# Ternary weights of the feed-forward layer: W2's blocks compared, turned and stored in the second turn of the loop, W1's in the first, and the order of every turn rewritten

## The chip, the core and the metric

The kernel runs on one core of a Trainium2 chip. It is written in Bass with an explicit program for each engine: TensorE (PE), VectorE (DVE), ScalarE (ACT), GpSimd (POOL) and SyncE (SP), which issues all transfers. The engines meet through semaphores only, and each runs its own list in the order in which it is written. The metric is the device time of one execution in microseconds (us).

## The reference

A transformer block on `x` (8 sequences, 1024 positions, 512 channels, float32), with layer norms behind each half. The first half is segmented attention with a compressive memory over segments of 128 positions (8 heads of 64 channels):

```python
q, k, v = xs @ Wq, xs @ Wk, xs @ Wv          # by segment of 128 positions
sq = elu(q_s) + 1.0
att_mem = sq @ mem / (sq @ z)
sk = elu(k_s) + 1.0
mem = mem + einsum('bhlk,bhlv->bhkv', sk, v_s)
z = z + sk.sum(axis=-2)
att = softmax(q_s @ k_s.T * scale) @ v_s
att = gate * att_mem + (1 - gate) * att
x = layernorm(x + att @ Wo)
```

The second half is a feed-forward layer whose weights (W1 2048x512, W2 512x2048) are ternary:

```python
def _quantize(W):
    gamma = mean(abs(W))
    return clip(round(W / (gamma + 1e-5)), -1.0, 1.0)
h = relu(x @ _quantize(W1).T + b1)
x = layernorm(x + h @ _quantize(W2).T + b2)
```

## The kernel before

**Tiling.** There are 32 groups of work (`NG`); a group is one segment of 128 positions of two sequences (`TG = 2`; the two are called t = 0 and 1). The main loop of each engine runs g = 0 to 33 and is software-pipelined. A pass of it, here called a turn, handles three groups: q, k and v projections, scores, softmax and the product with v (`attend`) of group g; the output projection with Wo and the layer norm of group g-1 (`project_out`, `residual`, `normalise`); and the feed-forward layer of group g-2, except its first up projections, which stand ahead of that at the end of the turn before. Products are kept accurate by splitting float32 operands into a high and a low float16 part and adding three matmuls; splitting is what most of the work on DVE, ACT and POOL is (`qk_split`, `v_split`, `p_split`, `xt_lo`, `w_split`, `h_split` with `h_rest`).

**Banks.** PE's results go to eight PSUM banks. `ffn_up` alternates between banks 0 and 1, `ffn_down` accumulates in banks 6 and 7, all other jobs take banks 2 to 5 in rotation (`take`), and each waits until the bank's last user on another engine is done.

**Memory.** `read_memory(g, t)` multiplies sq of group g with the memory that group g-2 left; `update_memory(g, t)` multiplies sk and v of a group and `mem_add` on DVE adds the result. sk reaches its layout by transfers: DVE transposes 32x32 pieces, and then `move_sk` on SP moves them in 16 transfers of 32 KB. `move_att` and `move_y` do the same for the mixed attention (ahead of Wo) and the normalised rows (y, ahead of the feed-forward layer). So SP issues 48 such transfers a turn, besides x, results and the detour of the group's largest value over DRAM (`amax_dram`, `amax_row`). SP is one queue: what stands behind `move_y` waits for its 16 issues.

**The ternary weights.** W1 and W2 stay in float32 in parts of `w2t`, `w1t` and `arena` until their thresholds are known. They are turned in 32 blocks of 128x512, 16 of W1 and 16 of W2. For block n, `compare(n)` writes two float16 masks, `wbelow` (weight under minus the threshold) and `wabove`; `turn_w(n)` on PE multiplies each 128x128 piece with the identity and with minus the identity, which gives the transposed ternary block in bank n % 2; `put_w(n)` on ACT stores it in `w1t` or `w2t`. The masks lie in `yt`, which holds the transposed y from the end of the first turn on, four blocks deep. DVE makes both masks of even blocks and the `above` mask of odd ones; POOL makes the `below` mask of odd ones. Blocks 0 to 15 are turned at the end of turn 0, blocks 16 to 31 in turn 1 up to the second k projection, all in banks 0 and 1, and the first up projection waits for all of them:

```python
if n >= 2:
    pe.wait_ge(sem["relu"], n - 1)
else:
    pe.wait_ge(sem["wput"], NBLOCKS)
pe.wait_ge(sem["yt"], by_t(g, 1))
```

**Order.** It is written out by hand in the five `for g in range(NG + 2)` loops; there is no planner.

## Time and profile before

| quantity | value |
| --- | --- |
| median of 3 runs | 1914.51 us (1912.84 to 1919.87) |
| profiled execution | 1912.87 us |
| its span in the profile | 1910.9 us |
| busy share of the span: PE, DVE, ACT, POOL | 97%, 76%, 53%, 42% |
| mean granted TensorE clock | 0.991 of full speed |
| transfers | 117.49 MB, mean 61 GB/s, q1 busy 29.4% of 16 engines' span |

The profiled execution is 1.64 us under the median of the runs shown, and its span is 1.97 us shorter than its time. All stretches below are in us from the start of the span. Busy shares are averages over a loop in which an engine may wait in one place and be the limit in another, so the text reads stretches and single instructions beside them. An instruction's record in the timeline gives its start, its duration and in brackets how long the engine was idle ahead of it and what ended this wait.

### The profile page before, as it was taken

The page shows a single profiled execution, that of the slowest core. Times are in us where ns is not written, and L with a number is a line of the kernel's source. Part 1 is how long each engine was busy: PE and PEld are TensorE (multiplying, and loading weights), DVE is VectorE, ACT ScalarE, POOL GpSimd, SP SyncE. Part 2 cuts the span into 40 slices and gives each one's busy share as a digit, 9 for nine tenths or more (in the row PEclk, how much of TensorE's full clock was granted, in tenths as well). Part 3 has the DMA queues.
Part 4 walks back from the last instruction along what each step waited for, and adds up shares of the span by engine and source line. Part 5 has one row for each costly group of instructions (what it writes and reads, how often), then busy time and mean ns, then how long its engine had stood idle before and what let it go on. Part 6 is the DMA issues. An engine that isn't in the chain of part 4 may idle for free.

```text
span 1910.9 us, 44707 instructions
## 1 busy us (share of the span) xinstructions
PE 1855.7 (97%) x16575; PEld 1311.8 (69%) x16575; DVE 1449.1 (76%) x2969; ACT 1006.1 (53%) x2426; POOL 794.7 (42%) x790
## 2 busy tenths in 40 slices
PE   5689999999999999999999999999999999999998
PEld 3566677766777766677766677766677766677765
DVE  7867777777777787777777877777777777777774
ACT  5755555555554555554555554545555645555541
POOL 1813344443344444344444344444345444344443
PEclk9889999999999999999999999999999999999999
DMA  8412333223333233233223333323333322333110
GB/s 270 123 23 46 58 61 66 52 49 59 62 59 65 49 53 61 58 60 65 54 45 64 61 59 64 64 38 60 61 59 63 67 38 59 61 58 62 36 23 23
DMA packets 556422, 117.49 MB, mean 61 GB/s; under 512 B 529824, under 2 KB 533808, under 8 KB 555696
## 3 DMA queue, kind: packets, MB, share of 16 engines
q1 hardware_dynamic: 556208, 114.64, 29.4%
q8 instruction: 134, 2.20, 0.6%
q14 instruction: 80, 0.66, 0.2%
HBM read 50.54 MB, written 16.80 MB: 35 GB/s over the span
## 4 chain that ended last, share of the span: by engine, by line
PE 80%; SPq 7%; DVE 6%; DMA 3%; issue 2%; ACT 1%; POOL 1%; DVEq 0%; POOLq 0%; ACTq 0%
PE bank L431 12%; PE bank L430 12%; PE bank L444 8%; PE bank L445 8%; SPq L1551 7%; PE bank L280 6%; PE bank L282 6%; PE bank L281 6%; PE bank L413 3%; PE bank L411 3%; PE bank L412 3%; PE bank L368 3%; DMA amax_row<-amax_dram 2%; PE bank L294 2%; PE bank L347 2%
## 5 line engine op out<-in xcount | busy, mean ns | idle before, releaser
L430 PE MATMUL bank<-yt,w1t 128*128 128x256 f16 x2048 | 453.9, 273 | 0.0
L431 PE MATMUL bank<-yt,w1t 128*128 128x256 f16 x2048 | 453.9, 273 | 0.0
L1141 ACT ACTIVATE prob<-bank,exp_bias,gscalars 128x128 f32<-128x128 f32 x512 | 227.6, 455 | 356.6 <-DVE exp_bias L723 347.7
L444 PE MATMUL bank<-w2t,arena 128*128 128x512 f16 x1024 | 388.4, 379 | 0.0
L445 PE MATMUL bank<-w2t,arena 128*128 128x512 f16 x1024 | 388.1, 379 | 0.0
L1187 ACT ACTIVATE arena<-bank,b_scaled,wscalars 128x256 f32<-128x256 f32 x512 | 262.9, 569 | 213.4 <-PE bank L431 156.3
L858 DVE CAST arena<-arena 128x512 f16<-128x512 f32 x256 | 154.8, 605 | 89.9 <-ACT arena L1187 89.1
L1317 POOL TENSOR_TENSOR att_mem<-att_mem,gate_in 128x512 f32<-128x512 f32 x60 | 83.1, 1385 | 330.1 <-DVE att_mem L762 318.7
L430 PEld LDWEIGHTS bank<-yt,w1t 128*128 128x128 f16 x2048 | 200.5, 98 | 23.3 <-issue 0.3
L431 PEld LDWEIGHTS bank<-yt,w1t 128*128 128x128 f16 x2048 | 200.3, 98 | 22.7
L1395 POOL TENSOR_TENSOR arena<-arena 128x512 f16<-128x512 f32 x128 | 155.3, 1213 | 87.6 <-DVE arena L858 87.6
L444 PEld LDWEIGHTS bank<-w2t,arena 128*128 128x128 f16 x1024 | 100.1, 98 | 111.9
L445 PEld LDWEIGHTS bank<-w2t,arena 128*128 128x128 f16 x1024 | 100.2, 98 | 110.5
L1353 POOL TENSOR_TENSOR at<-att_dot,at 128x512 f16<-128x512 f32 x60 | 89.7, 1495 | 191.3 <-ACT at L1160 191.3
L673 DVE SCALAR_TENSOR_TENSOR xt<-x_blocks,gscalars,xt 128x512 f16<-128x512 f32 x62 | 83.3, 1343 | 84.7 <-ACT xt L1095 84.7
L280 PE MATMUL bank<-xt,wk_hi 128*128 128x256 f16 x512 | 141.0, 275 | 0.0
L281 PE MATMUL bank<-xt,wk_hi 128*128 128x256 f16 x512 | 140.6, 275 | 0.0
L282 PE MATMUL bank<-xt,wk_lo 128*128 128x256 f16 x512 | 140.6, 275 | 0.0
L280 PE MATMUL bank<-xt,wq_hi 128*128 128x256 f16 x512 | 139.5, 273 | 0.0
L282 PE MATMUL bank<-xt,wq_lo 128*128 128x256 f16 x512 | 139.5, 273 | 0.0
L281 PE MATMUL bank<-xt,wq_hi 128*128 128x256 f16 x512 | 139.5, 273 | 0.0
L718 DVE TENSOR_REDUCE row_max<-bank 128x4 f32<-128x512 f32 x128 | 87.4, 683 | 37.6 <-PE bank L317 37.6
(191 smaller groups left out, 4392.9 us busy)
## 6 DMA issues: line engine op xcount, KB each, us to landing
rows<-in_L_attn_x SPq DMA_DIRECT2D x32, 512.0 KB, 3.6
out_rows<-rows SPq DMA_DIRECT2D x64, 256.0 KB, 2.3
x_blocks<-in_L_attn_x SPq DMA_DIRECT2D x248, 64.0 KB, 2.8
sk<-sk_t SPq DMA_DIRECT2D x480, 32.0 KB, 2.0
att_dot<-att_mem SPq DMA_DIRECT2D x480, 32.0 KB, 2.0
y_blocks<-rows SPq DMA_DIRECT2D x480, 32.0 KB
arena<-in_L_ffn_W SPq DMA_DIRECT2D x6, 1024.0 KB, 5.5
w2t<-in_L_ffn_W SPq DMA_DIRECT2D x2, 1024.0 KB, 13.3
```

The source lines that it names most:

```text
L280: pe.matmul(ps[:, :, c], w_hi[n][:, k, cols], xt[:, :, k], start=k == 0, stop=False)
L281: pe.matmul(ps[:, :, c], w_hi[n][:, k, cols], xt[:, :, KT + k], start=False, stop=False)
L282: ins = pe.matmul(ps[:, :, c], w_lo[n][:, k, cols], xt[:, :, k], start=False, stop=k == KT - 1)
L430: pe.matmul(ps[:, c], w1t[:, k, cols], yt[:, g % 2, :, k], start=k == 0, stop=False)
L431: ins = pe.matmul(ps[:, c], w1t[:, k, cols], yt[:, g % 2, :, KT + k], start=False, stop=k == KT - 1)
L444: pe.matmul(banks[own][:], h_hi[:, f, toks], w2t[:, f, :], start=f == 0, stop=False)
L445: ins = pe.matmul(banks[own][:], h_lo[:, f, toks], w2t[:, f, :], start=False, stop=f == FT - 1)
L858: dve.tensor_copy(hi, h32[:, n % NH32]).then_inc(sem["h_hi"], 1)
L1141: ins = act.activation(prob[:, t, at], ps[:, c], ACT.Exp, scale=gcol(g, G_EXP), bias=exp_bias[:, t, at:at + 1], accum_out=row_sum[:, t, h: ...
L1187: ins = act.activation(h32[:, n % NH32, c * GT:(c + 1) * GT], ps[:, c], ACT.Relu, scale=w(H_SCALE_Y), bias=b1_scaled[:, f:f + 1])
L1395: pool.tensor_tensor(lo, h32[:, n % NH32], hi, ALU.subtract).then_inc(sem["h_pool"], 1)
L1551: sp.dma_start(to, at).then_inc(done, 16)
```

## The change

What it does:

- `compare(n)` runs on DVE alone, for both masks of every block. POOL's comparisons go. One semaphore, `masks`, counts finished blocks.
- The masks are two blocks deep instead of four and lie in `yt[:, 1]` only; `yt[:, 0]` is free for the y of group 0.
- Blocks 0 to 15 (W1) are still turned at the end of turn 0 through banks 0 and 1. Blocks 16 to 31 (W2) go through banks 6 and 7, which `ffn_down` does not need before turn 2: 16 to 19 behind the first k projection of turn 1, 20 to 23 behind its two `project_out`, ahead of `scores(1, 0)`, 24 to 27 behind `turn_p(1, 0, 0)`, and 28 to 31 in turn 2, ahead of `ffn_up(0, 3)`.
- The first up projection waits for the 16 stores of W1 alone; the first `ffn_down` waits for all 32.
- The order of the turns is rewritten on every engine and for all 34 turns. On PE three up projections of group g-1 and both `update_memory(g, ...)` close a turn; before, one up projection stood there and `update_memory(g - 1, ...)` stood behind `ffn_up(g - 2, 4)` of the next turn. On SP the gates' return, two of W2's loads and the x of groups 3 and 4 move from the end of turn 0 into turn 1.

The diff, cut to its core (of the rewritten loops it shows only the end of PE's and one place of SP's):

```diff
-        wbelow = yt[:, 0].rearrange("p t k n -> p (t k n)").rearrange("p (b n) -> p b n", b=4)
-        wabove = yt[:, 1].rearrange("p t k n -> p (t k n)").rearrange("p (b n) -> p b n", b=4)
+        masks = yt[:, 1].rearrange("p t k n -> p (t k n)").rearrange("p (m b n) -> p m b n", m=2, b=2)
+        wbelow, wabove = masks[:, 0], masks[:, 1]
...
+        def turned_bank(n):
+
+            return banks[n % 2 if n < NBLOCKS // 2 else 6 + n % 2][:].rearrange("p (j c) -> p j c", j=4)
+
...
             def turn_w(n):
 
-                ps = banks[n % 2][:].rearrange("p (j c) -> p j c", j=4)
+                ps = turned_bank(n)
                 if n == 0:
                     pe.wait_ge(sem["ident16"], 1)
                 if n >= 2:
                     pe.wait_ge(sem["wput"], n - 1)
-                pe.wait_ge(sem["above"], n + 1)
-                pe.wait_ge(sem["below_pool" if n % 2 else "below"], n // 2 + 1)
+                if n == NBLOCKS // 2:
+                    pe.wait_ge(sem["hscale"], 1)
+                    pe.wait_ge(sem["thr_chain"], 2)
+                pe.wait_ge(sem["masks"], n + 1)
                 for j in range(4):
                     cols = slice(j * P, (j + 1) * P)
-                    pe.matmul(ps[:, j], wabove[:, n % 4, cols], ident16[:], start=True, stop=False)
-                    ins = pe.matmul(ps[:, j], wbelow[:, n % 4, cols], minus16[:], start=False, stop=True)
+                    pe.matmul(ps[:, j], wabove[:, n % 2, cols], ident16[:], start=True, stop=False)
+                    ins = pe.matmul(ps[:, j], wbelow[:, n % 2, cols], minus16[:], start=False, stop=True)
                 ins.then_inc(sem["wturn"], 1)
 
             def project_qk(g, n, j):
...
                 else:
-                    pe.wait_ge(sem["wput"], NBLOCKS)
+                    pe.wait_ge(sem["wput"], NBLOCKS // 2)
...
+                if g == 0 and piece == 0:
+                    pe.wait_ge(sem["wput"], NBLOCKS)
...
                 ffn_up(g - 1, 0)
+                ffn_up(g - 1, 1)
+                ffn_up(g - 1, 2)
+                update_memory(g, 0)
+                update_memory(g, 1)
...
+                if n == 0:
+                    dve.wait_ge(sem["masks"], NBLOCKS)
...
-                if n >= 4:
-                    dve.wait_ge(sem["wturn"], n - 3)
-                if n % 2 == 0:
-                    dve.tensor_scalar(wbelow[:, n % 4], src, w(BELOW[m]), None, ALU.is_lt).then_inc(sem["below"], 1)
-                dve.tensor_scalar(wabove[:, n % 4], src, w(ABOVE[m]), None, ALU.is_gt).then_inc(sem["above"], 1)
+                if n >= 2:
+                    dve.wait_ge(sem["wturn"], n - 1)
+                dve.tensor_scalar(wbelow[:, n % 2], src, w(BELOW[m]), None, ALU.is_lt)
+                dve.tensor_scalar(wabove[:, n % 2], src, w(ABOVE[m]), None, ALU.is_gt).then_inc(sem["masks"], 1)
...
-                else:
+                elif g == 1:
                     act.wait_ge(sem["wturn"], NBLOCKS)
...
                     act.wait_ge(sem["hscale"], 1)
+                    act.wait_ge(sem["masks"], NBLOCKS // 2 + 4)
...
-            def compare(n):
-                m, i, b = block_place(n)
-                src = ffn_raw(m, i)[:, b * 512:(b + 1) * 512]
-                if n in (1, 17):
-                    pool.wait_ge(sem["threshold"], m)
-                pool.wait_ge(*ffn_raw_loaded(m, i))
-                if n >= 4:
-                    pool.wait_ge(sem["wturn"], n - 3)
-                pool.tensor_scalar(wbelow[:, n % 4], src, w(BELOW[m]), None, ALU.is_lt).then_inc(sem["below_pool"], 1)
...
                     last = 4 * i + 3
-                    sp.wait_ge(sem["above"], last + 1)
-                    sp.wait_ge(sem["below"], last // 2 + 1)
-                    sp.wait_ge(sem["below_pool"], last // 2 + 1)
+                    sp.wait_ge(sem["masks"], last + 1)
...
                 if g == 1:
+                    gates_back()
+                    load_ffn_w(2, 2)
                     load_ffn_w(2, 3)
```

What the rewriting moves on DVE, in three places. The first is the first turn, between the splits of the q projection and those of Wv's last part. `wv_lo` is the low part of Wv (two halves), `row_max` and `exp_bias` belong to the softmax of group 0; rows of before first, then of now.

```order
L890 SCALAR_TENSOR_TENSOR wv_lo<-arena,wscalars,wv_hi 128x4x256
L872 TENSOR_REDUCE wscalars<-bank 1x1
L874 TENSOR_SCALAR wscalars<-wscalars 1x1
L876 TENSOR_SCALAR wscalars<-wscalars 1x1
L878 TENSOR_SCALAR wscalars<-wscalars 1x1
L686 SCALAR_TENSOR_TENSOR q_lo<-bank,q_hi 128x2x256
L693 SCALAR_TENSOR_TENSOR sq_t<-exp_tmp,relu_tmp 128x2x256
L890 SCALAR_TENSOR_TENSOR wv_lo<-arena,wscalars,wv_hi 128x4x256
L884 COPY wscalars<-bank 128x1
L885 RECIPROCAL wscalars<-bank 128x1
L718 TENSOR_REDUCE row_max<-bank 128x4
```

```order
L692 SCALAR_TENSOR_TENSOR q_lo<-bank,q_hi 128x2x256
L699 SCALAR_TENSOR_TENSOR sq_t<-exp_tmp,relu_tmp 128x2x256
L898 SCALAR_TENSOR_TENSOR wv_lo<-arena,wscalars,wv_hi 128x4x256
L692 SCALAR_TENSOR_TENSOR q_lo<-bank,q_hi 128x2x256
L699 SCALAR_TENSOR_TENSOR sq_t<-exp_tmp,relu_tmp 128x2x256
L946 TENSOR_SCALAR gate_cols<-gate_cols 128x4
L948 RECIPROCAL gate_cols<-gate_cols 128x4
L950 TENSOR_SCALAR gate_cols<-gate_cols 128x4
L724 TENSOR_REDUCE row_max<-bank 128x4
L729 TENSOR_SCALAR exp_bias<-row_max,gscalars 128x4
L898 SCALAR_TENSOR_TENSOR wv_lo<-arena,wscalars,wv_hi 128x4x256
L608 TENSOR_REDUCE amax<-x_blocks 128x1
```

The one-element chain (L872 to L878) and its spread (L884, L885) now stand ahead of these rows, and both q splits, the gates' three operations and the first softmax maxima now stand ahead of Wv's second half, on which the v projection waits.

The second place is turn 1, where group 0's rows are normalised; L840 before and L846 now is `normalise`, L858 and L866 are `h_split` (the rounding of a piece of the feed-forward layer's h), L602 and L608 the group's largest value. In turn 1 that h belongs to no group yet, so the rows are those of turn 2 on. Before, then now:

```order
L822 SCALAR_TENSOR_TENSOR rows<-bank,gscalars,rows 128x512
L831 BN_STATS stats<-rows 128x6
L833 BN_AGGR mean_var<-stats 128x2
L858 CAST arena<-arena 128x512
L718 TENSOR_REDUCE row_max<-bank 128x4
L723 TENSOR_SCALAR exp_bias<-row_max,gscalars 128x4
L602 TENSOR_REDUCE amax<-x_blocks 128x1
L840 TENSOR_SCALAR rows<-rows,mean_var,rstd 128x512 x2
L718 TENSOR_REDUCE row_max<-bank 128x4
```

```order
L828 SCALAR_TENSOR_TENSOR rows<-bank,gscalars,rows 128x512
L837 BN_STATS stats<-rows 128x6
L839 BN_AGGR mean_var<-stats 128x2
L724 TENSOR_REDUCE row_max<-bank 128x4
L729 TENSOR_SCALAR exp_bias<-row_max,gscalars 128x4
L846 TENSOR_SCALAR rows<-rows,mean_var,rstd 128x512
L608 TENSOR_REDUCE amax<-x_blocks 128x1
L846 TENSOR_SCALAR rows<-rows,mean_var,rstd 128x512
L724 TENSOR_REDUCE row_max<-bank 128x4
L729 TENSOR_SCALAR exp_bias<-row_max,gscalars 128x4
L866 CAST arena<-arena 128x512
```

The `h_split` that stood ahead of the softmax maxima and `normalise` now stands behind the second pair of maxima, and one `normalise` goes ahead of the group's largest value, the other behind it.

The third place is the same turn ahead of the two `attend`. L847 before and L853 now are `turn_y`, which transposes y's pieces once `move_y` has landed; L732 and L738 are `p_split`, whose `pt_lo` `attend` needs; L739 and L745 invert the softmax sums; L615, L623, L621 and L629 are the scale of the next x. Before, then now:

```order
L739 RECIPROCAL inv_sum<-row_sum 128x8
L746 TENSOR_SCALAR dot_scale<-inv_sum,gscalars 128x8 x2
L847 STREAM_TRANSPOSE y_blocks<-y_blocks 128x512
L615 TENSOR_REDUCE gscalars<-amax_row 128x1
L732 SCALAR_TENSOR_TENSOR pt_lo<-bank,pt_hi 128x512
L623 TENSOR_SCALAR gscalars<-gscalars 128x1
L847 STREAM_TRANSPOSE y_blocks<-y_blocks 128x512
L732 SCALAR_TENSOR_TENSOR pt_lo<-bank,pt_hi 128x512
```

```order
L853 STREAM_TRANSPOSE y_blocks<-y_blocks 128x512 x2
L745 RECIPROCAL inv_sum<-row_sum 128x8
L621 TENSOR_REDUCE gscalars<-amax_row 128x1
L738 SCALAR_TENSOR_TENSOR pt_lo<-bank,pt_hi 128x512
L629 TENSOR_SCALAR gscalars<-gscalars 128x1
L745 RECIPROCAL inv_sum<-row_sum 128x8
L752 TENSOR_SCALAR dot_scale<-inv_sum,gscalars 128x8
L633 TENSOR_SCALAR gscalars<-gscalars 128x1
L738 SCALAR_TENSOR_TENSOR pt_lo<-bank,pt_hi 128x512
```

Both `turn_y` now stand together, ahead of the inverted sums, the scale's chain and the last three `p_split`; before, the second stood between `p_split` rows.

## Rows read from the trace of the kernel before

**Rows 1.** Busy time by stretch; columns in its first row (PEclk: granted clock).
```profile
core 0: us, PE busy (x) PEld busy (x) DVE busy (x) ACT busy (x) POOL busy (x), PEclk, DMA share, GB/s
120.00:131.00 11.00, 7.73 (x72) 6.67 (x73) 7.27 (x20) 6.90 (x22) 0.46 (x1) 0.53 0.26 46
300.00:400.00 100.00, 100.00 (x926) 72.63 (x924) 77.31 (x153) 52.40 (x126) 42.77 (x43) 1.00 0.31 59
```

**Rows 2.** Timeline of PE: the memory read between the two attends, in three turns.
```profile
357.68 0.33 PE L368 MATMUL bank<-mem,sq_t 64*128 64x65 f32 x2
414.44 0.33 PE L368 MATMUL bank<-mem,sq_t 64*128 64x65 f32 x2
1785.13 0.33 PE L368 MATMUL bank<-mem,sq_t 64*128 64x65 f32 x2
```

**Rows 3.** The waits of PE: line, releaser, us in total, times, longest.
```profile
PE bank L368 <- DVE pt_lo L732: 3.9, 11, 0.4
PE bank L265 <- POOL yt L1405: 2.8, 9, 0.6
```

**Rows 4.** SyncE issuing transfers: two turns, y by line (ns), the page for sk.
```profile
396.46 10.43 SPq L1551 DMA_DIRECT2D y_blocks<-rows  x16
407.63 12.00 SPq L1563 DMA_DIRECT2D sk<-sk_t  x16
453.22 14.46 SPq L1551 DMA_DIRECT2D y_blocks<-rows  x16
468.42 11.11 SPq L1563 DMA_DIRECT2D sk<-sk_t  x16
...
L1551 SPq DMA_DIRECT2D y_blocks<-rows x480: 585/611/4204, 167.7 to 1832.1; - x160
...
sk<-sk_t SPq DMA_DIRECT2D x480, 32.0 KB, 2.0
```

**Rows 5.** Timeline, VectorE and GpSimd, ahead of the transfer of y.
```profile
393.22 1.16 POOL L1395 TENSOR_TENSOR arena<-arena 128x512 f16<-128x512 f32 x1
393.30 1.10 DVE L723 TENSOR_SCALAR exp_bias<-row_max,gscalars 128x4 f32<-128x4 f32 x1
...
395.45 0.99 DVE L840 TENSOR_SCALAR rows<-rows,mean_var,rstd 128x512 f32<-128x512 f32 x2
...
397.17 0.23 DVE L723 TENSOR_SCALAR exp_bias<-row_max,gscalars 128x4 f32<-128x4 f32 x1
```

**Rows 6.** The memory updates by line, 340 to 480; min/median/max ns, first and last start.
```profile
L399 PE MATMUL bank<-v,sk x64: 220/222/271, 368.3 to 426.0; 128*64 128x65 f32 x64
```

**Rows 7.** Timelines of the start: VectorE, ScalarE, then PE to the first up projection.
```profile
39.47 1.27 DVE L890 SCALAR_TENSOR_TENSOR wv_lo<-arena,wscalars,wv_hi 128x1024 f16<-128x1024 f32 x1
...
41.68 1.13 ACT L1194 ACTIVATE wo_hi<-arena,wscalars 128x1024 f16<-128x1024 f32 x1
...
39.19 0.29 PE L313 MATMUL bank<-k_hi,q_hi 64*128 64x128 f16 x2 [3.54 <-DVE q_lo L686]
...
41.10 0.61 PE L294 MATMUL bank<-wv_hi,xt 128*128 128x512 f16 x1
...
87.44 0.27 PE L280 MATMUL bank<-xt,wk_hi 128*128 128x256 f16 x1
...
108.81 0.38 PE L411 MATMUL bank<-wo_hi,at 128*128 128x512 f16 x1
...
110.20 0.23 PE L313 MATMUL bank<-k_hi,q_hi 64*128 64x128 f16 x2
...
130.65 0.27 PE L430 MATMUL bank<-yt,w1t 128*128 128x256 f16 x1
```

**Rows 8.** The comparisons by line; durations are min/median/max in ns.
```profile
L913 DVE TENSOR_SCALAR yt<-w2t,wscalars x8: 469/478/903, 58.9 to 66.3; 128x512 f16<-128x512 f32 x8
...
L1405 POOL TENSOR_SCALAR yt<-arena,wscalars x12: 1717/1982/2355, 68.1 to 94.1; 128x512 f16<-128x512 f32 x12
```

**Rows 9.** The stores of the turned W1, ScalarE, same columns.
```profile
L1215 ACT ACTIVATE w1t<-bank x16: 587/597/617, 63.5 to 78.8; 128x512 f16<-128x512 f32 x16
```

More of the change, by code:

```diff
@@ L28 @@
     ident half ident16 ones bload bias_load b2_load
-    wmax wrow wchain wall wscale wsplit_hi wsplit wscaled wsplit_pool thr_row thr_all thr_chain threshold wsum above below below_pool
+    wmax wrow wchain wall wscale wsplit_hi wsplit wscaled wsplit_pool thr_row thr_all thr_chain threshold wsum masks
     wturn wput bias_turn bias_col bias_max bias_row bias_cell bias_all hs_chain hscale gate_exp gate_chain gate_cols gate_there gates
@@ L503, in _ @@
             for g in range(NG + 2):
-                ffn_up(g - 2, 1)
                 if g == 0:
                     turn_max(1)
-                ffn_up(g - 2, 2)
+                    turn_bias()
+                if g == 2:
+                    for n in range(28, 32):
+                        turn_w(n)
                 ffn_up(g - 2, 3)
+                if g == 1:
+                    sum_all(2)
                 if g == 0:
                     spread_max(1)
+                project_qk(g, "k", 0)
+                if g == 0:
+                    turn_max(2)
+                ffn_up(g - 2, 4)
+                if g == 0:
+                    spread_max(2)
                 if g == 1:
@@ L513, in _ @@
                         turn_w(n)
-                ffn_up(g - 2, 4)
-                update_memory(g - 1, 0)
-                update_memory(g - 1, 1)
+                ffn_up(g - 2, 5)
+                project_qk(g, "k", 1)
+                turn_att(g - 1, 0)
+                project_qk(g, "q", 0)
+                turn_att(g - 1, 1)
+                project_qk(g, "q", 1)
+                if g == 0:
+                    turn_max(3)
+                ffn_up(g - 2, 6)
+                if g == 0:
+                    spread_max(3)
+                ffn_up(g - 2, 7)
+                project_out(g - 1, 0)
+                project_out(g - 1, 1)
                 if g == 1:
@@ L519, in _ @@
                         turn_w(n)
-                project_qk(g, "k", 0)
-                if g == 0:
-                    turn_max(2)
-                ffn_up(g - 2, 5)
-                if g == 0:
-                    turn_bias()
+                scores(g, 0)
+                ffn_down(g - 2, 0, 0)
+                project_v(g, 0)
+                project_v(g, 1)
+                turn_p(g, 0, 0)
                 if g == 1:
@@ L575, in _ @@
                 if g == 0:
-                    for n in range(4, 8):
+                    for n in range(12, 16):
                         turn_w(n)
@@ L1023, in _ @@
                         compare(n)
-                invert_sums(g, 1)
-                scale_sums(g, 0)
-                scale_sums(g, 1)
+                read_scale(g, 0)
+                residual(g - 2, 0, 1)
                 turn_y(g - 1, 0)
+                if g == 0:
+                    scalars(0, 3)
+                turn_y(g - 1, 1)
+                if (g + 1) % (LIVE * NSEG) < LIVE and LIVE * NSEG <= g + 1 < NG:
+                    reset_memory((g + 1) // (LIVE * NSEG), place(g + 1)[2])
+                invert_sums(g, 0)
                 all_max(g + 1)
-                p_split(g, 0, 1)
-                x_scale(g + 1, 0)
                 if g == 0:
@@ L1033, in _ @@
                         compare(n)
-                turn_y(g - 1, 1)
+                p_split(g, 0, 1)
+                x_scale(g + 1, 0)
+                invert_sums(g, 1)
+                yt_lo(g - 1, 0)
+                scale_sums(g, 0)
+                x_scale(g + 1, 1)
                 if g == 0:
```

300 lines of the change are left out of this document (121 added, 179 removed).

## The prediction

> **What bounds the kernel now.** I read the page first: PE is busy 97% of the span, so the time is PE's list plus its gaps. The stretches say where gaps can be: between 300 and 400 us PE is busy all of 100.00 us at full clock while DVE has 77.31 and ACT 52.40, but from 120 to 131, just ahead of the first up projection, it is busy 7.73 of 11.00 at a granted clock of 0.53 [rows 1]. So a change of order can win or lose in two places: at the start, where PE waits, and in the few turns where the steady loop stalls.
>
> How much the loop stalls comes from one PE instruction seen turn by turn. The memory read starts at 357.68 and 414.44, a turn of 56.76 us, and 25 turns after the first it starts at 1785.13 [rows 2]. 25 undisturbed turns would be 1419.0, the trace has 1427.45: 8.5 us of stalls, about 10 over the whole loop (32 turns against 25 give 10.8; the early ones have no y to move, so I take 9.9). The list of waits has 3.9 us in 11 of them at that read, for DVE's `pt_lo` [rows 3]; the rest is at the attend just ahead. What makes DVE late is SP: moving y takes 10.43 us in a good turn and 14.46 in a bad one [rows 4], DVE waits in line for it (`turn_y`), and `p_split` stands behind that. A single issue of these 480 takes 0.611 us by the median and 4.2 at most [rows 4]: some issues are slow for a reason the order does not touch. I count 11 turns with a slow y.
>
> **The change, part by part.** All sums are made against the profiled execution, 1912.87 us (span 1910.9 and 2.0 around it); the median of the runs shown lies 1.64 higher, and I add that at the end.
>
> *Fewer blocks ahead of group 0's output projection.* A block is 8 matmuls of 128 columns. Six matmuls of 512 columns take 1.39 us from 108.81 to the scores at 110.20, 0.23 with the drain and 0.22 without [rows 7], so 128 columns take 0.055 and a block 0.44. Of blocks 16 to 31, twelve leave the stretch ahead of `project_out(0, ...)`: 12 x 0.44 = 5.3. PE's waits for POOL's masks, 2.8 us in 9 [rows 3], go too, since the masks come from DVE; I take 2.6 of them there. Group 0's output projection would end 7.9 earlier than the 110.20 of now, at 102.3, if everything ahead were unmoved; the next two paragraphs come out even on that point, since the stores that gate it lose 0.6 and the k projections gain this in the same wait.
>
> *The same work comes back.* Blocks 20 to 23 now stand ahead of `scores(1, 0)` and 24 to 27 ahead of `scores(1, 1)`. DVE needs two comparisons of 0.478 us for each block [rows 8], 0.96 against PE's 0.44, and the masks are two deep, so the last two of four blocks are waited for: 4 x 0.44 + 2 x (0.96 - 0.44), some more for ACT's store (0.60 [rows 9]) ahead of bank 6's reuse, in all 3.5 for the first four, and 1.4 for the second, whose masks are partly made while PE has other work. Lead left: 4.4 at `scores(1, 0)`, 3.0 at `scores(1, 1)`. I carry 3.1 to the first up projection, 130.65 [rows 7] to about 127.5: that stretch waits for normalise, its transfer and DVE, not for PE. Blocks 28 to 31 ahead of `ffn_up(0, 3)` give back 2.8: four blocks at 0.44 plus the masks' lag 1.04. Sum from there: -0.3.
>
> *DVE and the v projection of group 0.* The second half of Wv's split, now at 39.47, gets behind both q splits and the first softmax maxima, and the last q split behind ScalarE's two Wo halves of 1.13 [rows 7]. Scores move from 39.19 to about 41.5, they take 1.5, maxima and bias 1.0, the split 1.27: the v projection starts at 45.3 instead of 41.10, 4.2 late. It costs the stores 1.9 at their start (the first is at 63.5 [rows 9]) since a softmax group of four exponentials now goes behind the first four stores, and 0.6 at the end, which is the part already counted. If that cover is missing, the 4.2 go through to the end.
>
> *POOL's comparisons.* A comparison on POOL takes 1.98 us by the median, on DVE 0.478 [rows 8]. 16 more on DVE are 7.7 us; DVE has room for it in turn 1, where no feed-forward work of an older group exists, save in the masks' lag above. DVE's port is a cost the other way: `exp_bias` takes 1.10 us beside POOL's `h_rest` and 0.23 without it [rows 5]. So DVE's own comparisons get faster too: their longest is 903 ns, near double the median [rows 8].
>
> The Trainium skill ("Advanced Engine Details and Errata", VectorE Performance Modes, Mode Summary) says that VectorE's second SBUF port is shared with GPSIMD and that the two block each other; the 1.10 against 0.23 agrees. By that rule alone every comparison on DVE that took 903 ns beside POOL's would come to 478, and the start would gain where PE waits for masks; by the rows PE waits there for POOL's masks, which are counted already, so the sum stays.
>
> *The steady turn.* Two things pull against each other. First, `h_split` and the slow `exp_bias` stood ahead of `normalise` at 395.45 [rows 5]; with `h_split` behind, y's transfer is issued about 1.0 us earlier (0.87 of it the slow `exp_bias`; what `h_split` frees and what the group's maximum, now between the two `normalise`, takes are about equal). In slow turns the stall was about 0.9 (9.9 over 11), so nearly all of that goes: -9.9. Second, `update_memory` stands closer to the transfer it needs. Now five up projections of 16 matmuls of 256 columns (0.109 each, 1.745 together) lie between the attends and the update, which starts at 368.3, 10.7 behind the read at 357.68 [rows 2, 6]. After the change there are three: 10.7 - 3.5 = 7.2, so in the turn of 414.44 PE comes to the update at 421.6. sk lands then: y's issues start at 395.45, take 10.43, the gap to sk's is 0.74, sk's issues take 11.11 to 12.00 (11.4), and the last lands 1.4 behind their end (2.0 from an issue of 0.611) [rows 4]: 419.4. The margin is 2.1 us in a good turn. In a turn with a slow y the lateness over 2.1 is a wait on PE: 14.46 - 10.43 = 4.0 in the one shown, so 1.9 there, and 0.4 to 1.7 in the others, 10.6 in all. Net +0.7. Bounds: -9.9 if sk is never late, +25 if the margin is not there (below).
>
> *Tail.* The last two `normalise` and transfers of results are issued back to back; half an issue, +0.3.
>
> Nothing else has a price: SP's loads of W2 and of x move later into turn 1, where its queue has 11 us of room ahead of their use, and the wait of `ffn_down` for all 32 stores comes 10 us behind the last one. If either were late it would show as a wait of PE at `ffn_down(0, 0, 0)`, up to 3 us once.
>
> Sum: -0.3 + 0.7 + 0.3 = +0.7, 1913.6 for the profiled execution, and with the 1.64 of the medians 1915.2; I say 1915.0.
>
> **Rivals.** *Faster, 1903.* The lead of 7.9 is kept from Wo's end to the first up projection, as the comparisons run beside other work, less 2.8 for the last blocks, and a part of the stalls goes because slow issues have more room: -5.1 - 4.5 - 1.6 for a warm clock in the 11 us ahead of the first up projection [rows 1] is -11.2 from 1914.5, 1903. For it: the low clock there comes with PE's gaps, and shorter gaps end both. Against: that stretch waits for a chain of DVE and SP that the change moves by 1 us only.
>
> The Trainium skill ("TensorE: Matmul & The Clock Gate", Why this matters for your kernels) warns that idle gaps between bursts take TensorE back to half clock; the 0.53 from 120 to 131 agrees. Blocks strewn through turn 1 could by that rule fill gaps (the faster rival) or, where PE waits for masks ahead of them, make new ones.
>
> *Slower, 1937: `update_memory` waits for sk in every turn.* The place is PE's L405, the first matmul of the update at the turn's end. It decides as soon as the path of y and sk is over 2.1 us longer than I have it. A good turn's y at 10.43 and sk at 12.00 already take 0.6 of that; `yt`'s last reader, the x of the next group or 1.5 us of DVE's `sk_t` transpose behind `h_split` would take the rest. Then each turn is 0.8 to 0.9 longer, 28 turns: +24 on the profiled 1912.9, 1937. For it: sk's 16 issues begin where SP is free, so there is no slack in SP. Against: in the turn of 396.46 the margin is counted on real rows.
>
> *Slower at the start, about 1923.* DVE becomes the bound in turns 0 to 2: all 64 comparisons at 0.478 are 30.6 us on it, and PE at half clock ahead of the first up projection pays double for its own work: +8. This is inside "same" by the bound below.
>
> *The change does not do what it says:* the three banks' waits serialise the W2 blocks with `ffn_down`. No `ffn_down` exists before turn 2, so I give it nothing.
>
> **How the numbers follow.** About 0.5%, 9.6 us, is what a measurement of this kernel can tell from no change. The likeliest case (start about even, stalls traded) has 0.48, the start's rival with +8 has 0.08: 0.56 same. The faster rival has 0.21, the wait for sk in every turn 0.23. The range is 1902, just past the faster rival, to 1933, where the sk wait costs 0.6 a turn; the likeliest case alone spans 1908 to 1922.
>
> **What would show it.** The first up projection at 127.5 (130.65 before); v's projection at 45.3; no wait of PE for POOL in the turning of blocks; the memory read at a distance of 56.76 in good turns; no or few waits of the read for `pt_lo`; and waits of PE at the update for the transfer of sk, in about 11 turns and of 10 us in all. If that last number is over 25, the slower rival holds; if it is under 3 and the attends do not wait either, the faster one. A start later than 134 means that the comparisons on DVE, or v, set its end.

## The result

| | kernel before | changed kernel |
| --- | --- | --- |
| median of 22 runs each | 1915.62 us | 1919.78 us |
| lowest and highest | 1911.72, 1920.33 | 1916.16, 1923.48 |
| ratio, 95% interval | | 1.0021 (1.0013 to 1.0030) |
| profiled execution, span | 1912.87, 1910.9 | 1917.00, 1915.0 |
| mean granted clock | 0.991 | 0.990 |

The change makes the kernel slower by 0.21%, 4.2 us. It is under the 0.5% that the prediction took for no change, and with 22 runs on each side it is clear of zero. The two profiled spans differ by 4.1 us, so the trace pair can be read for where they go. The memory read between the attends marks three stretches:

| | before | after | difference |
| --- | --- | --- | --- |
| v projection of group 0 | 41.10 | 46.03 | +4.9 |
| first store of a W1 block | 63.5 | 68.4 | +4.9 |
| last store of a W1 block starts | 78.8 | 82.4 | +3.6 |
| output projection of group 0 ended, next work of PE | 110.20 | 107.51 | -2.7 |
| first scores of turn 1 | 110.20 | 110.52 | +0.3 |
| first up projection | 130.65 | 132.21 | +1.6 |
| memory read of turn 2 | 185.75 | 190.86 | +5.1 |
| the same 28 turns later | 1785.13 | 1787.56 | +2.4 |
| end of the span | 1910.9 | 1915.0 | +4.1 |

In this pair of profiles the start loses 5.1, the loop gives back 2.7, the last turns lose 1.7. A second pair (experiments 5 and 6) has +2.2, -5.1 and +1.6 for the three: single profiles, which show where time goes, while the 4.2 us is the medians'.

### The profile after

The busy time by stretch, which answers to [rows 1]; the second stretch holds the first three up projections:

```profile
core 0: us, PE busy (x) PEld busy (x) DVE busy (x) ACT busy (x) POOL busy (x), PEclk, DMA share, GB/s
120.00:131.00 11.00, 6.88 (x86) 5.68 (x85) 8.71 (x22) 7.64 (x24) 0.00 (x0) 0.81 0.34 83
132.20:137.50 5.30, 5.30 (x46) 4.47 (x44) 5.26 (x7) 2.33 (x5) 2.54 (x2) 0.86 0.22 36
300.00:400.00 100.00, 99.89 (x927) 72.90 (x926) 79.74 (x163) 52.50 (x122) 45.12 (x45) 1.00 0.32 60
```

The clock ahead of the first up projection is 0.81 where it was 0.53, but the next stretch still has 0.86: from 132.21 to the memory update at 138.27 the three up projections take 6.1 us, in the turn of 361.34 5.3 (363.09 to 368.43). The loop is as full as before; DVE has 2.4 us more in these 100 us.

The start, which answers to [rows 7] and [rows 9]; DVE, then SyncE, ScalarE and its stores by line, then PE, and last its waits from 64.9 to 107.2:

```profile
41.73 1.92 DVE L950 TENSOR_SCALAR gate_cols<-gate_cols 128x4 f32<-128x4 f32 x1
...
45.95 0.34 SPq L1495 DMA_DIRECT2D arena<-in_L_ffn_W  x1
46.34 0.44 SPq L1499 DMA_DIRECT2D gate_dram<-gate_cols  x1
47.09 0.33 SPq L1511 DMA_DIRECT2D amax_dram<-amax  x1
57.48 0.32 SPq L1518 DMA_DIRECT2D amax_row<-amax_dram  x1
57.85 0.47 SPq L1495 DMA_DIRECT2D arena<-in_L_ffn_W  x1
...
66.05 1.91 ACT L1212 ACTIVATE rows<-arena 128x2048 bf16<-128x2048 f32 x1 [2.09 <-DMA arena<-in_L_ffn_W]
...
L1222 ACT ACTIVATE w1t<-bank x16: 586/597/632, 68.4 to 82.4; 128x512 f16<-128x512 f32 x16
...
46.03 0.59 PE L300 MATMUL bank<-wv_hi,xt 128*128 128x512 f16 x1 [3.50 <-issue]
...
107.51 0.22 PE L271 MATMUL bank<-ident,yt 128*128 128x128 f16 x1 [0.53 <-DVE yt L920]
...
110.52 0.23 PE L319 MATMUL bank<-k_hi,q_hi 64*128 64x128 f16 x2
...
132.21 0.40 PE L436 MATMUL bank<-yt,w1t 128*128 128x256 f16 x1
...
PE bank L271 <- ACT w1t L1222: 3.7, 3, 2.2
PE bank L271 <- DVE yt L920: 2.9, 11, 0.4
```

The gates' last tiny operation takes 1.92 us at 41.73, and the v projection follows Wv's split at 46.03. On SyncE, the load of W2's second part (57.85) is issued right behind the return of the group's maximum (57.48), and ScalarE's last sum starts at 66.05 after 2.09 us of waiting for this load. All 16 stores of W1 are behind that sum. The first W2 blocks on PE's way to the scores begin at 107.51, where the output projection has ended; the scores start 3.0 us later. The last two lines are waits inside the blocks ahead of that, for ScalarE's stores and for VectorE's masks. In the kernel before, the same stretch has 0.9 us of waits for stores, 2.8 for GpSimd's masks and 1.5 more at the same line (L265) with no releaser named.

The reads of memory, which answer to [rows 2]:

```profile
361.34 0.33 PE L374 MATMUL bank<-mem,sq_t 64*128 64x65 f32 x2
418.11 0.33 PE L374 MATMUL bank<-mem,sq_t 64*128 64x65 f32 x2
1787.56 0.33 PE L374 MATMUL bank<-mem,sq_t 64*128 64x65 f32 x2
```

A good turn is 56.77 us long as before. From the read of turn 2, 28 turns take 1596.70 us; 28 of 56.765 would be 1589.42. The excess is 7.3, where the kernel before has 9.96 (1599.38). Without their excess the two spans are 1900.9 and 1907.7, in the second pair 1902.1 and 1906.0. Taken from the medians of 22 runs (less the 2.0 us outside the span), that leaves about 12 us of stalls for the kernel before and 11 for the changed one. This is an estimate, and by it the loop gives back about 1 us, less than either pair shows.

The waits of PE from 140 us on, which answer to [rows 3]:

```profile
PE bank L405 <- issue: 3.9, 7, 0.8
PE bank L417 <- DVE at L806: 1.3, 1, 1.3
...
PE bank L388 <- issue: 0.8, 2, 0.4
PE bank L405 <- DVE att_dot L780: 0.8, 1, 0.8
```

The waits for `pt_lo` at the read (L368 before, L374 now), 3.9 us in 11, are gone from the list. In their place PE waits 4.7 us in 8 at the memory update (L405) and 0.8 at the attend. The list names no releaser for 7 of the 8 (`issue`), but in 9 of the 28 turns the update starts 0.09 us after sk's last transfer has landed; in the turn of 361.34, which is not held up, it starts 1.97 us after it (368.43 and 366.46). L417 is the last group's `project_out`: VectorE's `at_lo` now comes behind one `h_split` more, 1.3 us once, which is most of the tail's loss.

VectorE ahead of y's transfer, which answers to [rows 5], then SyncE, which answers to [rows 4]:

```profile
396.77 0.54 DVE L846 TENSOR_SCALAR rows<-rows,mean_var,rstd 128x512 f32<-128x512 f32 x1
...
398.35 0.54 DVE L846 TENSOR_SCALAR rows<-rows,mean_var,rstd 128x512 f32<-128x512 f32 x1
...
399.63 0.23 DVE L729 TENSOR_SCALAR exp_bias<-row_max,gscalars 128x4 f32<-128x4 f32 x1
399.76 0.42 DVE L866 CAST arena<-arena 128x512 f16<-128x512 f32 x1
```

```profile
398.92 10.42 SPq L1526 DMA_DIRECT2D y_blocks<-rows  x16
410.08 12.99 SPq L1538 DMA_DIRECT2D sk<-sk_t  x16
L1526 SPq DMA_DIRECT2D y_blocks<-rows x480: 585/611/4122, 171.7 to 1833.7; - x160
```

The memory read of this turn is at 418.11, and y's issues start 19.19 ahead of it; before, 414.44 less 396.46 was 17.98. y is issued 1.2 us earlier. `exp_bias` takes 0.23, since `h_split` (L866) and so GpSimd's `h_rest` come behind it. The slow issues are still there: one of them took 4.1 us. They stand at fixed places: in all 14 traces of this document, from at least three chips, the same 12 of the 30 transfers of y (groups 1, 2, 6, 9, 13, 14, 15, 20, 21, 22, 27 and 28) hold an issue of over 2 us. Only how long they take varies.

The comparisons, which answer to [rows 8]:

```profile
L920 DVE TENSOR_SCALAR yt<-w2t,wscalars x8: 478/480/483, 63.6 to 73.5; 128x512 f16<-128x512 f32 x8
```

With no GpSimd work beside them these take 478 to 483 ns; the longest before took 903. Here the trace agrees with what the Trainium skill states ("Advanced Engine Details and Errata", VectorE Performance Modes, Mode Summary): VectorE's second SBUF port is shared with GPSIMD, and GPSIMD's instructions and VectorE's two-port ones block each other; no row here shows the ports themselves. The gates' 1.92 us fits as well: it started at 41.73 and ended with GpSimd's split of Wo (41.50, 2.12 us). And the 24 comparisons of the blocks in `arena` are not all free of it: their median is 480 ns too, but the one at 88.27, beside GpSimd's mixing of the attention (88.04, 1.44 us), took 1496.

### The profile page after: what moved, and what is told of

Its sections match the earlier page's. It is cut to its first block, busy times and chain, and to the rows that moved or that the text cites. A ratio compares the mean times of both kernels' runs of the same rounds, so it can differ in the third digit from the quotient of the medians.

```text
span 1915.0 us, 44689 instructions
## 1 busy us (share of the span) xinstructions
PE 1853.6 (97%) x16575; PEld 1310.5 (68%) x16575; DVE 1476.1 (77%) x2985; ACT 1010.4 (53%) x2426; POOL 777.3 (41%) x774
## 4 chain that ended last, share of the span: by engine, by line
PE 89%; DVE 5%; SPq 2%; DMA 2%; issue 1%; ACT 1%; POOL 0%; POOLq 0%; DVEq 0%; ACTq 0%
PE bank L436 12%; PE bank L437 11%; PE bank L452 11%; PE bank L453 10%; PE bank L286 6%; PE bank L287 6%; PE bank L288 6%; PE bank L374 3%; PE bank L417 3%; PE bank L419 3%; PE bank L418 3%; PE bank L353 3%; PE bank L301 2%; PE bank L300 2%; PE bank L302 2%; SPq L1526 2%
## 5 line engine op out<-in xcount | busy, mean ns | idle before, releaser
L1364 POOL TENSOR_TENSOR at<-att_dot,at 128x512 f16<-128x512 f32 x60 | 80.8, 1346 | 373.9 <-ACT at L1166 373.9
L1328 POOL TENSOR_TENSOR att_mem<-att_mem,gate_in 128x512 f32<-128x512 f32 x60 | 89.3, 1489 | 291.5 <-DVE att_mem L768 291.5
L1406 POOL TENSOR_TENSOR arena<-arena 128x512 f16<-128x512 f32 x128 | 150.5, 1176 | 112.6 <-DVE arena L866 112.6
L869 DVE TENSOR_TENSOR arena<-arena 128x512 f16<-128x512 f32 x128 | 124.2, 970 | 4.4
L738 DVE SCALAR_TENSOR_TENSOR pt_lo<-bank,pt_hi 128x512 f16<-128x512 f32 x128 | 86.9, 685 | 43.2 <-ACT pt_hi L1158 43.1
```

Source lines behind the costliest of these rows:

```text
L869: dve.tensor_tensor(lo, h32[:, n % NH32], hi, ALU.subtract).then_inc(sem["h_dve"], 1)
L1328: pool.tensor_tensor(a, a, gate_in[:], ALU.mult).then_inc(sem["gated_in"], 1)
L1406: pool.tensor_tensor(lo, h32[:, n % NH32], hi, ALU.subtract).then_inc(sem["h_pool"], 1)
```

## The experiments

Profiles of one kernel differ, mostly in the stalls, so the start is read from PE's milestones and the stalls from the excess over 28 turns of 56.765 us. Experiments 1 to 4 ran on one chip, 5 to 8 on a second, 9 to 12 on a third. Experiments 7, 9 and 11 have several runs and an interval; the others are one run each, so their times prove nothing by themselves.

### 1. The kernel before, comparisons on VectorE alone

```diff
-                if n % 2 == 0:
-                    dve.tensor_scalar(wbelow[:, n % 4], src, ...).then_inc(sem["below"], 1)
+                dve.tensor_scalar(wbelow[:, n % 4], src, ...)
...
-                    compare(1)          # GpSimd, and its other 15
```

> The kernel before with both comparisons of every block on VectorE, four deep as they were; nothing else moved. Theory: GpSimd's comparisons cost PE 2.8 us of waits and slowed VectorE's own comparisons, so the first up projection comes 1 to 3 us earlier than 130.65, and this part of the change is a gain. Rival: VectorE's 7.7 us more work ends later in the first turn and the first up projection moves to 132 or later, which would make this the part that costs.

The first up projection is at 128.81, 1.8 earlier. This part of the change is a gain, with PE's waits for masks at 2.6 us (2.8 for GpSimd's before, 4.3 with the unnamed ones at the same line). Its time (1926.94 in one run, 1917.16 for before beside it) says something else: the excess of this profile is 24.6 us, in the loop, where this edit changes nothing. Experiments 5 and 6 are for that.

### 2. The changed kernel, W1's masks four deep

```diff
+            if n < NBLOCKS // 2 and n % 4 >= 2:
+                return masks0[:, above, n % 2]      # in yt[:, 0]
+            return masks[:, above, n % 2]
```

> The changed kernel with W1's masks four blocks deep again, in both halves of yt; W2's stay two deep. Theory: PE's late start of the blocks (64.98 against 62.09) and ScalarE's stores set the pace, so the last W1 block and the first up projection (132.21) move by under 1 us. Rival: two deep masks are what made the 16 blocks end at 82.39, and they end 2 us or more earlier now.

Stores of W1 go from 68.2 to 80.8 instead of 68.4 to 82.4, and the first up projection comes at 130.96. Against the profiles with the same start (132.21, 130.94 in experiment 6 and 131.35 in experiment 7) that is 1.2, 0.4 or nothing. From the first store to the last it takes 12.6 us here and 14.0, 13.6 and 14.4 in those three, a gain of 1.0 to 1.7, between theory and rival: masks two deep cost something, but they aren't what made the start late.

### 3. The load of W2's second part ahead of the maximum's return

```diff
+                if g == 0:
+                    load_ffn_w(2, 1)
                 bounce_back(g + 1)
-                if g == 0:
-                    load_ffn_w(2, 1)
```

> The changed kernel with SyncE issuing the load of W2's second part ahead of the return of the group's maximum instead of behind it. Theory: that load is issued at 57.85 only because it is queued behind the return (57.48), which waits for a small transfer that sits behind a 1 MB load; ScalarE's last sum then waits for it until 66.05 with all stores behind it. Expected: load issued at about 49, the sum at 64.0, the first store about 2 us earlier than 68.44, the first up projection 1 to 2 us earlier than 132.21. Rival: the load only shares its bandwidth with the other and lands as late, or the stores are held by the masks; then nothing moves.

SyncE, ScalarE's stores and PE's first up projection of this kernel:

```profile
47.62 0.33 SPq L1511 DMA_DIRECT2D amax_dram<-amax  x1
49.23 0.33 SPq L1495 DMA_DIRECT2D arena<-in_L_ffn_W  x1
58.34 0.32 SPq L1518 DMA_DIRECT2D amax_row<-amax_dram  x1
...
L1222 ACT ACTIVATE w1t<-bank x16: 592/597/632, 65.6 to 79.3; 128x512 f16<-128x512 f32 x16
...
129.08 0.27 PE L436 MATMUL bank<-yt,w1t 128*128 128x256 f16 x1
```

Two lines moved, and the load is issued at 49.23 instead of 57.85, the first store comes at 65.6, and the first up projection 1.9 to 3.1 us earlier. The last sum no longer waits: the load landed at 60.04, 6.0 us earlier, though it took 10.8 us instead of 8.2, and the sum starts at 63.25. The theory holds, with one part of it wrong: see 4.

### 4. Wv's second split first

```diff
                     w_split("v", 0)
+                    w_split("v", 1)
                 qk_split(g, "q", 1)
...
-                    gates()        # now behind group_max(g + 1)
```

> The changed kernel with the second half of Wv's split on VectorE ahead of the last split of q, and the gates' three operations behind the group's maximum. Theory: the v projection starts at about 42.6 instead of 46.03, the load into Wv's place is issued at about 40.5 instead of 45.95, the first store comes 3 to 5 us earlier than 68.44 and the first up projection 2 to 4 us earlier than 132.21. Rival: the late v split is covered by other work, as the sum of the prediction had it, and the first up projection stays within 1 us of 132.21.

SyncE, then ScalarE's last sum:

```profile
40.38 0.34 SPq L1494 DMA_DIRECT2D arena<-in_L_ffn_W  x1
47.31 0.47 SPq L1510 DMA_DIRECT2D amax_dram<-amax  x1
57.88 0.32 SPq L1517 DMA_DIRECT2D amax_row<-amax_dram  x1
58.24 0.43 SPq L1494 DMA_DIRECT2D arena<-in_L_ffn_W  x1
...
65.82 1.91 ACT L1211 ACTIVATE rows<-arena 128x2048 bf16<-128x2048 f32 x1 [4.77 <-DMA arena<-in_L_ffn_W]
```

The v projection starts at 42.93, and the first up projection at 133.22. The theory fell: 3 us gained at v bring nothing, since the last sum now waits 4.8 us for the same load. And the 1 MB load into Wv's place, issued 5.6 us earlier here, did not make the maximum's return come earlier (57.88), so it isn't what holds the small transfer (47.31), as experiment 3's text had it. What makes that return 10.4 us late instead of 7.4 before stays open; the gates' transfer, now issued ahead of it and not behind, is the candidate, and was not tried. The trace of this experiment speaks rather against it: that transfer landed 1.6 us after its issue (8.2 in the changed kernel), and the return is as late.

### 5 and 6. Both kernels again, on one chip

> The kernel before, unchanged, for a second profile on the chip that runs the next three. The reads of memory in turns 2 to 30 had 9.96 us more than 28 turns of 56.765 in its first profile, the changed kernel 7.28. The runs of the first four experiments had 17.6 to 24.6 where the two kernels had 10.0 and 7.3. If that is the chip and its slow issues, this profile has 15 or more as well, at the attends and the read; if it is what the edits did, it has about 10.

> The changed kernel, unchanged, on the same chip. Theory: its stalls stand mostly at the memory update, and the excess over 28 turns is 0 to 4 us under that of the kernel before on this chip. Rival of the prediction (the update waits in every turn): excess 24 or more and over 20 turns longer than 56.77. The first up projection within 0.5 us of 132.21 would show how far the start repeats.

PE's waits from 140 us on, of the kernel before, then of the changed one:

```profile
PE bank L368 <- DVE pt_lo L732: 4.9, 13, 0.4
PE bank L382 <- issue: 4.6, 5, 1.5
```

```profile
PE bank L405 <- issue: 5.0, 7, 1.2
PE bank L388 <- issue: 1.9, 3, 0.7
...
PE bank L374 <- DVE pt_lo L738: 0.9, 1, 0.9
```

The excess is 14.98 before and 9.90 after: in both pairs of profiles the changed kernel stalls less, by 2.7 and 5.1 us. Whether chips or executions make the difference isn't shown. 17 other runs of the kernel before on this second chip go from 1911.44 to 1920.92, so one execution can have 9 us more than the next on the same chip, and the profile of experiment 5 (1919.06) lies at the upper end of these. The stalls of the four first experiments (17.6 to 24.6) stay open too: their runs took 1923.64 to 1932.14, and the one run of the unchanged kernel before on that chip 1917.16. The changed kernel was not run there. The start repeats to 1.3 us, worse than the 0.5 that I had expected: first up projections at 130.53 and 130.94, reads of turn 2 at 186.86 and 189.08.

### 7. The changed kernel, the updates one up projection later

```diff
                 ffn_up(g - 1, 2)
-                update_memory(g, 0)
-                update_memory(g, 1)
...
                 ffn_up(g - 2, 3)
+                update_memory(g - 1, 0)
+                update_memory(g - 1, 1)
```

> The changed kernel with both memory updates behind the fourth up projection instead of the third, and VectorE's two additions behind the third rounding of h. Theory: all waits of the update for sk (4.7 us in 8 turns in the first profile, more on a chip with slower issues) were 0.87 us or shorter and vanish, since PE comes 1.75 us later; the excess falls by 3 us or more and the time by 2 to 6 us against the changed kernel. Rival: what was waited for at the update is waited for at the next attend, since the slow y is behind both, and the excess stays.

PE's waits from 140 us on:

```profile
PE bank L388 <- issue: 1.4, 3, 0.8
...
PE bank L374 <- DVE pt_lo L738: 1.0, 1, 1.0
```

No wait at the update is left, and they did not come back at the attend (1.4 against 1.9). The excess is 3.63 against 9.90, in one profile each. The median is 1913.34, the ratio to before 0.9995 (0.9985 to 1.0006); the changed kernel has 1.0021. So where the update stands costs the change about 5 us (an estimate from the two ratios, which were not taken side by side).

### 8. Both start edits

> The changed kernel with both edits: the load of W2's second part issued ahead of the return of the maximum, and the second half of Wv's split first. Each alone moved the first up projection from 132.21 to 129.08 (load) and to 133.22 (split). Theory: the early split gave nothing because the last sum still waited 4.8 us for that load, so with the load early it pays: the first store at about 63.5, the first up projection at 126 to 127.5. Rival: the split's gain is lost elsewhere (the thresholds, PE at half clock in the gaps), and it stays at 129.

The first store is at 62.2, the first up projection at 126.24, the read of turn 2 at 184.17. Theory right: with the load out of the way the earlier split pays 2.8 us against experiment 3's 129.08, more than the 1.3 us by which a start repeats.

### 9. Four edits together

> The changed kernel with four edits at once: load of W2's second part first, Wv's second split first, W1's masks four deep, updates of the memory behind the fourth up projection. Theory: the start's gains add (first up projection 126.24 with the first two, 1 us less with the masks, so about 125; 132.21 and 130.94 without) and the loop keeps the 6.3 us that the late update gave on one chip. Expected time 7 to 11 us under the kernel before, ratio 0.9945 to 0.9965, faster than both kernels. Rival: the gains overlap, since both parts wait for the same SyncE queue, and the ratio is 0.998 or more.

Median 1907.36, ratio 0.9952 (0.9937 to 0.9967): 8.4 us less than before on this chip, faster than both kernels. The first up projection is at 124.56, the read of turn 2 at 182.58, the excess 4.75. Experiment 11 gets as much out of the kernel before with another edit, so this shows that the change's losses can be mended, not that the change is needed for the gain.

### 10. The last four blocks in turn 1

```diff
-                if g == 2:
+                if g == 1:                    # now behind turn_p(g, 1, 0)
                     for n in range(28, 32):
                         turn_w(n)
```

> The changed kernel with W2's blocks 28 to 31 compared, turned and stored in turn 1, where PE waits ahead of the last two turn_p (2.27 and 1.61 us), not in turn 2. Theory: PE has idle time there, so up to 2.9 us of block work costs nothing: the first up projection stays within 1 us of 132.21 or 130.94, and the memory read of turn 2 comes 2 to 3 us earlier than 190.86 or 189.08. Rival: VectorE and ScalarE are the ones that PE waits for there, their 3.2 and 2.4 us of block work push the softmax of the second sequence, the first up projection is 3 us later and the read no earlier.

PE's lines with a wait in this stretch:

```profile
125.65 0.63 PE L353 MATMUL bank<-ident,prob 128*128 128x128 f32 x4 [2.37 <-ACT prob L1147]
...
132.34 0.66 PE L342 MATMUL bank<-ident,rows 128*128 128x128 f32 x4 [1.18 <-DVE yt L812]
```

The first up projection comes at 134.59 and the read of turn 2 at 189.61, between the 190.86 and 189.08 of the unchanged order. The rival is nearer (the first up projection is 2.4 to 3.7 us later, the read in between): PE's idle time there was a wait for VectorE and ScalarE, and the blocks need just these two.

### 11. The kernel before, `h_split` behind the softmax maxima

```diff
-                h_split(g - 2, 7)
                 score_max(g, 0, 0)
...
                 score_max(g, 0, 1)
+                h_split(g - 2, 7)
```

> The kernel before with one thing of the steady order changed: VectorE's last rounding of h stands behind the second pair of softmax maxima instead of ahead of the first. Theory of the prediction: y is issued about 1 us earlier, so the stalls of the attends and the read (10 to 15 us in two profiles) shrink by half or more, ratio 0.996 to 0.998. Rival: those stalls come from the second transpose of y standing among the splits of p, and issuing y 1 us earlier helps little: ratio 0.999 to 1.001.

SyncE, VectorE and PE in the turn of [rows 5], then PE's waits from 140 us on:

```profile
395.44 10.41 SPq L1551 DMA_DIRECT2D y_blocks<-rows  x16
...
393.15 0.23 DVE L723 TENSOR_SCALAR exp_bias<-row_max,gscalars 128x4 f32<-128x4 f32 x1
394.42 1.00 DVE L840 TENSOR_SCALAR rows<-rows,mean_var,rstd 128x512 f32<-128x512 f32 x2
396.29 0.42 DVE L858 CAST arena<-arena 128x512 f16<-128x512 f32 x1
...
414.62 0.33 PE L368 MATMUL bank<-mem,sq_t 64*128 64x65 f32 x2
```

```profile
PE bank L368 <- DVE pt_lo L732: 1.5, 4, 0.4
PE bank L382 <- issue: 0.4, 1, 0.4
```

y is issued 19.18 us ahead of the read, as in the changed kernel, and `exp_bias` takes 0.23. The issues themselves are no faster (one of y's took 4.7 us here), so what changed is that PE is no longer held up by them. Waits at attend and read are 1.9 us instead of 9.5 in experiment 5, the excess is 2.71, and the median 1905.11: ratio 0.9939 (0.9924 to 0.9954), 10.7 us less than the kernel before beside it. Experiments 10 and 12, on the same chip and with the changed kernel's loop, have 12.15 and 12.5. One line moved on one engine gives as much as the four edits of experiment 9, and more than I had expected (0.996 to 0.998).

### 12. The changed kernel without W2's blocks

> The changed kernel without comparing and turning W2's 16 blocks (ScalarE's 16 stores stay and copy stored W1 blocks, so W2's product is not the reference's). Theory: on PE the 16 blocks and the waits inside them take 3.5, 3.6, 3.9 and 3.1 us at their four places, about 11 of it ahead of the first up projection; PE has waits of 4 us behind them which take up part, so the first up projection comes 5 to 8 us earlier and the read of turn 2 8 to 11 us earlier. Rival: the stretch ahead of the first up projection is bound by normalise, its transfer and VectorE, and the first up projection moves by under 2 us.

The first up projection is at 125.96, 6.3 earlier than 132.21, the read of turn 2 at 181.42, 9.4 earlier; against experiment 6 it is 5.0 and 7.7. So W2's blocks cost the start 8 to 9 us, with their comparisons on VectorE, which this edit takes out too. They are hidden in one place only: behind the output projection 8 blocks and the waits inside them take PE 6.2 us (8 x 0.44, 2.1 and 0.6), and from its end to the first up projection it is 3.1 us shorter here (103.80 to 125.96 against 106.98 to 132.21).

## Why the prediction was right, and where its sum was off

The time came 4.8 us over the forecast's 1915.0, inside its range and inside the 1908 to 1922 of the case that was called likeliest. Of that case "stalls traded" is right and "start about even" is not: the start lost 5.1 us (2.2 in the second pair). By its steps:

- *Fewer blocks ahead of the output projection*: predicted 7.9 earlier, measured 3.3 to its end (110.27 and 106.98), 2.7 to the next work of PE at 107.51. The 12 blocks did go. Of the 4.6 that are missing, 2.9 are PE's first block, which starts at 64.98 instead of 62.09, and 1.7 are the stretch from there to the end of the output projection, which is 6.2 shorter and not 7.9: PE waits 3.7 us there for ScalarE's stores, which stand behind the late sum (0.9 before). The clause that failed is that the stores "lose 0.6 at the end". They lost 3.6, and that was carried to the scores: predicted -4.4, measured +0.3. What blocks 20 to 23 add was right: 3.5 predicted; measured 3.0 from 107.51 to 110.52 and the 0.53 of wait ahead of it.
- *The v projection*: predicted 45.3, measured 46.03. The cover that I named, the softmax group moved behind the first stores, was there, but a term was missing: the load of W2's second part, ahead of which SyncE's queue holds the maximum's return. I had priced the load of W2 into Wo's place at nothing. Experiment 3 shows it (1.9 to 3.1 us for two lines), experiment 8 shows that the late v costs another 2.8 as soon as the load is early.
- *First up projection*: predicted 127.5 (the sum's own lead there was 3.0, I carried 3.1), measured 132.21 and 130.94. From there: predicted 2.8 for blocks 28 to 31, measured 2.9 from 139.35 to 142.28, where the next up projection starts, right. My point that the stretch ahead waits "not for PE" was half wrong: without W2's blocks and their comparisons that stretch is 3.1 us shorter, for 6.2 us less on PE (experiment 12).
- *POOL's comparisons*: predicted a gain of 2.6 from the masks' waits. With masks four deep experiment 1 has the first up projection 1.8 earlier. In the changed kernel, two deep, the waits for masks are 2.9 us where 2.8 were named and 1.5 more had no releaser named, a gain of 1.4 at most.
- *Steady turn*: y 1.0 us earlier predicted, 1.2 measured. The mechanism, `h_split` and `exp_bias` in front of `normalise`, is shown by experiment 11 alone; what each of the two gives wasn't separated. The -9.9 was the right size (excess 14.98 and 9.96 before, 2.71 in experiment 11). The wait that takes its place is at the update for sk, as forecast, in 8 turns, and for 4.7 us where 10.6 were forecast: y's extra time in a slow turn is less on average than the one shown. Experiment 6 has it at 5.0 us, and in experiment 7, where the update comes later, it is gone, does not come back at the attend, and the excess is 6.3 us less. Net predicted +0.7, measured -2.7 and -5.1 in the two pairs of profiles, about -1 by the medians.
- *Tail*: predicted +0.3, measured 1.7. I had looked at the last `normalise` and not at `at_lo`, which the same rewriting put behind one `h_split` more.

So the sum was off by 5.4 us in the start and 1.4 in the tail one way, and by 3.4 in the loop the other way (2.5, 1.3 and 5.8 in the second pair). That the loop's error took back most of the start's was luck: the start alone was off by more than the 4.8 us by which the time missed. The faster rival needed the lead at the output projection, which the late stores had eaten. The slower rival needed the wait for sk in every turn; the list has it in 8 of 28. The margin that the forecast put at 2.1 us in a good turn is 1.97 in the turn of 361.34.

## What to carry to other kernels

When one operation is put later, list every transfer that is allowed to start by it, what stands ahead of that transfer in its queue, and who waits for it to land: here the operation moved was on VectorE, the load stood in SyncE's queue, the sum that waited for it was ScalarE's, and PE paid 2 to 3 us. When a wait is removed by moving work, try the single move alone before the whole rewriting: one line cured more of the stalls than the rewriting of every turn did. And a profile's stalls that come from slow transfers have to be compared over several executions on one chip: 17 runs of the kernel before on one chip differed by 9.5 us, more than twice the whole change.

## What the runs showed of the hardware that I had not expected

The slow issues of SyncE's y transfers come in the same 12 of 30 transfers in all 14 traces, whatever the kernel and the chip, and what they cost varied: an excess of 9.96 and 14.98 us for the unchanged kernel before in two profiles, 24.6 with an edit that touches only the start. Whether the chip or the execution sets that stays open, and so does why these transfers are slow. A transfer of 0.5 KB to DRAM (`amax_dram`) takes 6.5 to 9.1 us to land in the kernel before, while 1 MB loads issued near the first one took 4.9 and 5.0; but a 1 MB load took 8.2 in the changed kernel (issued at 57.85, with sk's transfers right behind it) and 10.8 in experiment 3. So the small transfer's place in a queue matters as much as a load's for everything that waits behind it. Experiments 9 and 11 were not joined in one kernel: the start of 9 (first up projection 6 us earlier than before, read of turn 2 3 us) with the loop of 11 might be faster than either, but this was not run.
